# Moving low parts, first norms and row statistics on VectorE behind the gated products of the shared expert

## What is computed

```python
x = x + _L0_ffn_ref(_layernorm(x, axis=-1), ...)

def _L0_ffn_ref(x, gate_w, expert_fc1, expert_fc2, expert_proj,
                shared_fc1, shared_fc2, shared_proj, shared_gate_w):
    ...                                    # router, top 2 of 8 experts, their outputs summed in y
    s1 = xf @ shared_fc1.T                 # 512 -> 1408
    s2 = xf @ shared_fc2.T
    shared = jax.nn.silu(s1) * s2 @ shared_proj.T
    y = y + jax.nn.sigmoid(xf @ shared_gate_w.T) * shared
    return y.reshape(b, t, c)
```

## Time and profile before

| | |
|---|---|
| Median of three runs | 2281.58 us (2278.69 to 2283.24) |
| Profiled execution: its own time | 2282.07 us |
| Profiled execution: span on the core | 2280.3 us |
| TensorE busy | 2222.6 us, 97% |
| VectorE busy | 1433.0 us, 63% |
| ScalarE busy | 1042.5 us, 46% |
| GpSimd busy | 468.8 us, 21% |

### The profile page before, as it was taken

How to read it: one execution, slowest core, us unless ns; L and a number is a source line. 1 busy time by engine, 2 the same in 40 slices (tenths; PEclk the granted TensorE clock), 3 DMA queues, 4 the chain that set the end, 5 groups by cost and what they waited for, 6 DMA issues and landing times. The chain is left out here.

```text
span 2280.3 us, 32035 instructions
## 1 busy us (share of the span) xinstructions
PE 2222.6 (97%) x11033; PEld 1844.3 (81%) x11033; DVE 1433.0 (63%) x2984; ACT 1042.5 (46%) x1863; POOL 468.8 (21%) x445
## 2 busy tenths in 40 slices
PE   7999999998999999999999999999998999999999
PEld 5777778787999977888888888888877888888887
DVE  6854365545777767766777777676776555555544
ACT  5532120103566566666666666666664222323221
POOL 4433454501111162000100001000031202121000
PEclk9999999999999999999999999999999999999999
DMA  6431322114777785101110001101102223332331
GB/s 224 129 106 42 106 56 38 30 61 150 258 281 264 272 284 199 38 20 37 42 31 28 28 28 28 37 18 37 37 1 84 84 97 102 97 129 70 111 116 51
DMA packets 92027, 219.58 MB, mean 96 GB/s; under 512 B 9552, under 2 KB 30544, under 8 KB 88976
## 3 DMA queue, kind: packets, MB, share of 16 engines
q1 hardware_dynamic: 83680, 191.16, 24.6%
q0 software_dynamic: 8240, 27.01, 4.6%
HBM read 174.35 MB, written 43.78 MB: 96 GB/s over the span
## 5 line engine op out<-in xcount | busy, mean ns | idle before, releaser
L2112 ACT ACTIVATE route_weights<-route_weights,xa_minus_max 128x512 f32<-128x512 f32 x256 | 184.8, 722 | 194.3 <-DVE xa_minus_max L2263 194.2
L2279 DVE TENSOR_TENSOR xa_late_hi<-xa_ps_t,route_wv_hi 128x512 fp32r<-128x512 f32 x256 | 174.8, 683 | 130.6 <-ACT route_wv_hi L2121 130.5
L2050 POOL TENSOR_TENSOR route_kv_lo<-route_rows,route_kv_hi 128x1024 fp32r<-128x1024 f32 x32 | 76.9, 2404 | 708.2 <-ACT route_kv_hi L2086 708.1
L2121 ACT ACTIVATE route_wv_hi<-xa_ps_t 128x512 fp32r<-128x512 f32 x256 | 151.3, 591 | 106.8 <-PE xa_ps_t L2466 71.2
L2263 DVE CUSTOM_DVE_ANT_0 route_weights<-xa_ps_s,route_mask_bias 128x512 f32<-128x512 f32 x256 | 175.6, 686 | 0.9 <-issue 0.6
L2466 PEld LDWEIGHTS xa_ps_t<-ident,route_weights 128*128 128x128 f32 x1024 | 126.5, 140 | 42.7 <-issue 10.0
L2466 PE MATMUL xa_ps_t<-ident,route_weights 128*128 128x128 f32 x1024 | 153.7, 273 | 5.2 <-DVE xa_late_hi L2279 5.2
L2838 ACT ACTIVATE ffn_silu<-ffn_ps_gate,late_scales 128x512 f32<-128x512 f32 x64 | 44.0, 688 | 248.9 <-PE ffn_ps_gate L87 248.9
L85 PE MATMUL xa_ps_p<-route_wv_hi,route_kv_hi 128*128 128x512 f32 x288 | 119.3, 414 | 5.3 <-issue 3.0
L1046 ACT ACTIVATE moe_silu<-moe_ps_gate 128x512 f32<-128x512 f32 x44 | 26.2, 596 | 200.7 <-PE moe_ps_gate L87 200.6
L2654 DVE TENSOR_TENSOR route_kv_lo<-route_weights,route_kv_hi 128x1024 fp32r<-128x1024 f32 x42 | 53.7, 1279 | 101.7 <-ACT route_kv_hi L2649 101.6
(11 more groups left out here) (540 smaller groups left out, 6562.9 us busy)
## 6 DMA issues: line engine op xcount, KB each, us to landing
route_weights<-in_ffn_w SPq DMA_DIRECT2D x64, 512.0 KB, 3.7
route_weights<-in_expert_w SPq DMA_DIRECT2D x12, 1408.0 KB
route_weights<-wd_folded SPq DMA_DIRECT2D x64, 256.0 KB, 2.7
ex_w_raw<-in_expert_w SPq DMA_DIRECT2D x11, 1408.0 KB
moe_y<-ex_y SPq DMA_DIRECT2D x39, 256.0 KB, 3.5
route_weights<-in_expert_w SPq DMA_DIRECT2D x12, 768.0 KB
ex_w_raw<-in_expert_w SPq DMA_DIRECT2D x11, 768.0 KB
route_weights<-in_xa_w SPq DMA_DIRECT2D x16, 512.0 KB, 3.6
```

The costliest lines, as they stand in the source:

```text
L2050: pool.tensor_tensor(kvl[b % 2][:], rawkv[b % 2], f32(kvh[b % 2][:]), ALU.subtract).then_inc(M.kv_ready, 1)
L2112: act.activation(prob[slot][:], prob[slot][:], ACT.Exp, bias=nmx[:, slot:slot + 1], scale=-1.0, accum_out=tot[:, slot:slot + 1]).then_inc( ...
L2121: act.activation(PTh[:, :, tt * P:(tt + 1) * P], psT[tt % 2][:].rearrange("p (k n) -> p k n", k=TT), ACT.Copy).then_inc(M.pt_hi, 1)
L2279: dve.tensor_tensor(PTl[:, :, tt * P:(tt + 1) * P], psT[tt % 2][:].rearrange("p (k n) -> p k n", k=TT), f32(PTh[:, :, tt * P:(tt + 1) * P] ...
```

## The change

Three pieces of VectorE's order move. No instruction is added or removed, and the other engines' orders stay.

```diff
+        STATS_STEPS = {1: 2, 5: 3}
...
                 for t in range(TT, 2 * TT):
                     stats(t)
-                for t in range(2 * EARLY, 2 * EARLY + 2):
-                    prepare(t)
...
-                    if s in (1, 3):
-                        for t in range((s + 3) // 2 * TT, (s + 5) // 2 * TT):
+                    if s in STATS_STEPS:
+                        for t in range(STATS_STEPS[s] * TT, STATS_STEPS[s] * TT + TT):
                             stats(t)
...
                     for s in range(B * gc):
                         b, j = divmod(s, gc)
-                        if s < gc - (GC - 2):
-                            split_lo(g, GC - 2 + s)
-                        if b == B - 1 and j >= 2 and which != "last":
-                            split_lo(g + 1, j - 2)
...
                         dve.tensor_tensor(hlo[s % 2][:], hid[:], f32(hhi[s % 2][:]), ALU.subtract).then_inc(M.hidden_ready, 1)
+                        if which == "first" and s == 0:
+                            for t in range(2 * EARLY, 2 * EARLY + 2):
+                                prepare(t)
+                        if s < gc - (GC - 2):
+                            split_lo(g, GC - 2 + s)
+                        if b == B - 1 and j >= 2 and which != "last":
+                            split_lo(g + 1, j - 2)
                         if j == 0 and b >= 1:
                             add_x(b - 1)
```

## The result

The changed kernel takes **2270.85 us** (median of 5 executions, 2270.00 to 2272.16); the kernel before, in the same comparison, 2281.44 us (5 executions, 2275.78 to 2283.24). The ratio is 0.9962 (95%: 0.9949 to 0.9974), that is 8.7 us less (5.9 to 11.6). The profiled execution took 2270.20 us, its span is 2268.4 us. The prediction was 2269.8 us, a gain of 12.3 us, with a range of 2266 to 2275.

The account below looks back on a forecast made before the run. TensorE, busy for 97% of the span, bounds the kernel. Gains of 4.1, 1.26, 3.6 and 3.4 us sum to 12.3 us, taken from the profiled 2282.07 us: 2269.8 us, range 2266 to 2275.

Parts of the forecast that it names:

- The four places: TensorE's waits A, B, C and D in the shared expert, costing 7.77 us, 12.8 us with the slow clock.
- A: Row turn, first group's step 0: 2.3 us wait; norms and low parts behind the gated products gain 4.1 us.
- B: First product down of batch 1: 1.1 us wait; statistics of batch 3 two steps later gain 1.26 us.
- C: First product down of the middle group: wait goes with low parts behind the gated products, gaining 3.6 us.
- D: First product down of the last group: wait goes with low parts behind the gated products, gaining 3.4 us.
- The overlap term: At each of TensorE's four waits: the cost is its idle time plus 0.16 us of lost matmul overlap.
- The slow clock: Stretches of 8 us around A, C and D: granted clock 0.79 costs 1.68 us each, 5.04 us together.
- Rival 1: Middle and last group starts: wait moves to the weights' low parts; 7.3 us gained, 2274.8 us; chance 12%.
- signs of being wrong: `moe_ps_gate` waiting for weights' low parts, clock under 1.00 behind idle under 1 us, or a later stage losing the gain.
- Rival 2: GpSimd's fold delays gather and experts' start: decides from 16 us of lengthening, takes the whole gain at 28 us; chance 4%.
- Rival 3: Low parts late at all three group starts, slow clock each time: 2286.6 us or more; chance 3%.
- All later stages last as long as before: Stages behind the shared expert keep their lengths, while the shared expert's stage ends some 12 us earlier.

Follow-up runs that it names:

- C and D alone: Kernel before with only the low parts in steps 0 and 1 of the middle and last groups moved behind their gated products: 2277.63 us, ratio 0.9977.
- B alone: Kernel before with only the row statistics of the last batch moved from step 3 to step 5: 2278.24 us, one execution.

## Why the prediction came out, and which of its steps didn't

- **The four places**: right. All four waits went, each by the edit that the prediction assigned to it, and A, B and the pair C and D can be taken one by one: 3.9 us (1.4 to 6.6), 1.37 us (from the trace) and 5.2 us (3.0 to 7.3) add up to 10.5, against 8.7 and 10.0 for the whole in two comparisons. The low parts moved in steps 14 and 15 are in none of these parts; the stretches that hold them, from step 6 to step 15 of the first group (82.6 us) and from step 2 to step 15 of the middle group (108.0 us), last the same in all fourteen profiles, so they cost nothing, as predicted.
- **The overlap term** (a wait costs its idle time plus 0.16 us): B's stretch gave 1.37 to 1.39 us for 1.10 us of idle time, against 1.26; 0.1 us short. The first matmul behind a wait lasts 0.50 us, and the next starts 0.34 us after it instead of 0.23 (298.23 and 298.57 at C): this is what the term left out.
- **A**: 4.17 us for 4.1 in the first pair of profiles, with no residual at all. In the other profiles in which its order was that of before, A cost 1.9 to 2.5 us.
- **C and D**: 3.26 and 3.35 us for 3.6 and 3.4. The residuals I took, 0.2 us each, were 0.6 us at C (0.30 of it idle) and 0.35 at D, measured against the profile of "C and D alone", which had none: the bounds 0 to 1.0 held, with the low parts at 3.51 us.
- **The slow clock, 1.68 us at each of A, C and D: the step that failed, by its size.** It holds for the execution from which it was read. In the three profiles of the unchanged kernel the clock fell at A, C and D three times, once and not at all. With it, the idle times were those of one execution: the sum of the four in the three profiles is 7.13, 6.83 and 4.78 us. The stage of before was 12.2, 9.0 and 5.3 us longer than that of the changed kernel, 8.8 us on average. That, and not 12.3, agrees with the 8.7 and 10.0 us of the timed comparisons; 12.3 lies above the first interval and within the second (7.1 to 13.0). The executions without a profile say the same of the clock: in the second comparison the changed kernel's mean clock is 0.9974 and that of before 0.9960, and at 1.7 to 2.3 us for each 0.001 this is some 2.4 to 3.2 us of the 10.0, an estimate, where the sum had 5.04 us for it.
- **Why the time was right nevertheless**: the sum was made against the same profiled execution that it was read from, 2282.07 us. It was 0.2 to 1.4 us above the medians of before, and what the sum took off was what that execution had lost. The three profiled executions of before took 2278.9 us on average; less their 8.8 us that is 2270.1. The changed kernel has little left that can vary in this stage, so an execution of before less its own waits leads to its time. That is a reason for the time to come out near, and luck has its part in it: the gain was put 1.7 to 3.6 us too high and the start 0.2 to 1.4 us too high, and in the pair of profiles the 0.8 us gained ahead of the stage and the 1.0 us lost behind it, neither of them in the sum, cancel.
- **Rival 1** (the wait moves to the weights' low parts): its mechanism is there, at C, with 0.3 us of idle time and without a slow clock; so one of the prediction's signs of being wrong did appear, at a size within its own bounds. The 1.0 us did not come, because the fold never stood on everything at once: at C the products' high part kept its 0.43 us, and at D the low parts took 2.42 us.
- **Rival 2** (the fold becomes late): the last store was at 464.29 us for 466.9, the gather at 482.24 for 482.9. The deciding point was wrong, 16 us instead of about 45, since I took the start of the gather as the start of the path: behind it lay another 32 us.
- **Rival 3** (slower): nothing of it; three low parts never took more than 3.51 us.
- **"All later stages last as long as before"**: right to 0.3 us for the experts and the last stage. The cross-attention does not hold still: 927.9 to 928.8 us in the three profiles of before, 929.1 and 931.1 in two of the changed kernel, but also 931.6 without the fold in before's order and 928.0 with B alone. Part of it is the clock, which fell in it in the changed kernel's profiles and in one of three of before; between the first two profiles this is 1.4 us more, and all that stands ahead of it 0.6 us less. Whether the change itself lengthens the stage by a microsecond or two can't be settled from so few profiles; it stays open. So does where the clock falls in the executions of before that took longer than its profiled ones.

## What to carry to other kernels

Read a wait's size from more than one execution before it goes into a sum: here the same four waits of an unchanged kernel cost 5.3 to 12.2 us, and only where the work stood, not what it cost, was the same each time. An order in which the engine that bounds the kernel hangs on little work of another engine is worth more than its average says: in the two comparisons that have both, the changed kernel's five executions lay within 2.2 and 3.2 us of each other, those of before were spread over 7.5 us (five of them) and 9.4 us (17). And where a rival is "this becomes late", follow its slack to the instruction that stops the bounding engine, not to the next instruction in its own queue.

## What the runs showed of the hardware

- **The granted clock does not follow from the length of one idle time alone.** At A, C and D it fell behind idle times of 1.79, 1.92, 2.32, 2.90 and 3.12 us, and behind none of those of 0.97 to 1.54 us; but it also did not fall behind one of 1.86 us, at A of the second profile of before. Behind the 3.12 us the stretch of 8 us had 0.61 on average, behind the others 0.79. In the cross-attention the same wait of 2.37 us was followed by 1.00 in one execution and by 0.79 in another, and in the third profile of before the clock fell (0.79) behind a wait of 1.19 us.
- **VectorE and GpSimd lengthen each other's instructions to a like duration.** A low part of the weights (two inputs in SBUF) takes 0.63 us alone and 1.17 beside the fold; an addition of the fold 0.74 us alone and 1.06 to 1.19 beside it. GpSimd's root on 128x4 elements went from 1.04 to 1.32 us. A high part of the product (one input in SBUF) takes 0.43 us alone, 0.90 beside the fold's additions and 0.93 beside GpSimd's issue of a DMA.
- **The same DMA issue on SyncE's queue took from 0.42 to 1.06 us**, and what it fetched was in use 3.5 to 5.2 us after the stage's start. In the kernel before all of this was on TensorE's path; in the changed one only the two latest landings reached it, with 0.5 and 0.6 us.
